# Queries and keys of a window attention block made with the tokens in another order

## The reference, cut to what matters

```python
xn = layernorm(x, ln1_w, ln1_b)
xs = jnp.roll(xn, shift=(-3, -3), axis=(1, 2))
xw = xs.reshape(B, H//7, 7, W//7, 7, C).transpose(0, 1, 3, 2, 4, 5).reshape(-1, 49, C)
qkv = xw @ qkv_w + qkv_b                     # (windows, 49, 3*192)
q, k, v = ...                                # each (windows, 6 heads, 49, 32)
attn = softmax(jnp.einsum('bhqd,bhkd->bhqk', q, k) * scale)
o = jnp.einsum('bhqk,bhkd->bhqd', attn, v) @ proj_w + proj_b
x = x + roll(unwindow(o), (3, 3))
h = gelu(layernorm(x, ln2_w, ln2_b) @ mlp_w1 + mlp_b1)
x = x + (h @ mlp_w2 + mlp_b2)
```

## Time and profile before

| what | value |
|---|---|
| time before, median of 3 runs | 3240.66 us (3238.58 to 3244.01) |
| the profiled execution: its own time | 3234.78 us |
| its span, first to last instruction | 3233.0 us |
| mean granted TensorE clock | 0.995 of full speed |
| TensorE busy (matmuls) | 3174.8 us, 98% of the span |
| VectorE, ScalarE, GpSimd busy | 69%, 62%, 22% |
| one step of the loop | about 24.8 us |

### The profile page before, as it was taken

The page is one execution under the profiler, slowest core; times in us unless marked ns, Lnnn a source line. Parts: engine busy times, 40 slices in busy tenths (PEclk is TensorE's granted clock), DMA queues, the critical chain, the costliest instruction groups (busy, mean ns, idle before and its releaser), DMA issues.

```text
span 3233.0 us, 110732 instructions
## 1 busy us (share of the span) xinstructions
PE 3174.8 (98%) x43444; PEld 2651.3 (82%) x43444; DVE 2227.1 (69%) x5903; ACT 2020.4 (62%) x3595; POOL 696.9 (22%) x785
## 2 busy tenths in 40 slices
PE   6999999999999999999999999999999999999998
PEld 6888888888888888888888888888888888888886
DVE  4677667666766676677667766766677667666764
ACT  3666666666666666666666666666666666666665
POOL 1222222222222222222222222222222222222221
PEclk8999999999999999999999999999999999999999
DMA  1010001000100010001000100000010001000100
GB/s 44 24 28 24 22 22 28 24 22 22 29 23 22 24 27 23 22 25 27 23 22 25 27 22 22 26 26 22 22 28 25 22 22 28 24 22 22 28 24 17
DMA packets 112096, 79.78 MB, mean 25 GB/s; under 512 B 10079, under 2 KB 111553, under 8 KB 112065
## 3 DMA queue, kind: packets, MB, share of 16 engines
q1 hardware_dynamic: 112064, 79.35, 9.3%
HBM read 40.78 MB, written 38.54 MB: 25 GB/s over the span
## 4 chain that ended last, share of the span: by engine, by line
PE 95%; ACT 3%; issue 1%; POOL 0%; DVE 0%; DMA 0%; SPq 0%; POOLq 0%; DVEq 0%; ACTq 0%
PE ps L743 31%; PE ps L810 16%; PE ps L746 15%; PE ps L818 8%; PE ps L778 5%; PE ps L841 5%; PE ps L861 4%; ACT vt L618 3%; PE ps L706 3%; PE ps L827 2%; PE ps L714 2%; PE ps L826 2%; PE ps L716 1%; DMA xin<-in_x 0%; POOL xb L362 0%
## 5 line engine op out<-in xcount | busy, mean ns | idle before, releaser
L743 PE MATMUL ps<-zh,w 128*128 128x392 f32 x3072 | 666.8, 345 | 22.1 <-ACT vt L618 21.4
L743 PEld LDWEIGHTS ps<-zh,w 128*128 128x128 f32 x3072 | 535.9, 188 | 63.2 <-ACT vt L618 62.4
L810 PE MATMUL ps<-g,w 128*128 128x392 f32 x1536 | 562.4, 502 | 0.0
L630 ACT ACTIVATE yT<-ps,b 128x392 f32<-128x392 f32 x256 | 150.5, 588 | 468.5 <-PE ps L818 424.4
L810 PEld LDWEIGHTS ps<-g,w 128*128 128x128 f32 x1536 | 271.4, 190 | 151.3
L743 PE MATMUL ps<-zh,wqkv 128*128 128x400 f32 x1536 | 391.7, 363 | 0.0
L666 ACT ACTIVATE g<-ps,biasf 128x392 f32<-128x392 f32 x768 | 386.2, 567 | 3.0 <-PE ps L743 1.1
L743 PEld LDWEIGHTS ps<-zh,wqkv 128*128 128x128 f32 x1536 | 281.2, 190 | 79.6 <-issue 77.0
L370 POOL TENSOR_TENSOR ve<-mv,eps 98x4 f32<-98x4 f32 x256 | 51.0, 199 | 1340.7 <-DVE mv L404 1340.7
L253 POOL TENSOR_TENSOR prob<-prob,rcp 128x588 f32<-128x588 f32 x128 | 152.2, 1189 | 867.7 <-DVE rcp L523 867.7
L412 DVE TENSOR_SCALAR z<-x,mv,rs 98x192 f32<-98x192 f32 (+2 forms) x768 | 208.6, 343 | 186.5 <-POOL rs L372 186.5
(11 more groups left out here) (94 smaller groups left out, 6021.0 us busy)
## 6 DMA issues: line engine op xcount, KB each, us to landing
xin<-in_x SPq DMA_DIRECT2D x128, 147.0 KB
out<-yo SPq DMA_DIRECT2D x128, 147.0 KB
xin<-in_x SPq DMA_DIRECT2D x128, 71.2 KB
out<-yo SPq DMA_DIRECT2D x128, 71.2 KB
xin<-in_x SPq DMA_DIRECT2D x128, 54.8 KB
out<-yo SPq DMA_DIRECT2D x128, 54.8 KB
xin<-in_x SPq DMA_DIRECT2D x128, 18.8 KB
out<-yo SPq DMA_DIRECT2D x128, 18.8 KB
```

The lines of the kernel that those rows point to most:

```text
L743: last = pe.matmul(dst, cols(w, part), act_ if zh is zh2 else windows(act_, WIDE, EVEN), start=(n == 0), stop=(n == 4))
L810: last = pe.matmul(ps[:, Y[0], 0:M], w2[:, k, 0:A], g[:, k, :], start=(k == 0), stop=(k == KC - 1))
```

## The change

The tokens of q and k get another order. In the moving operand of `qk` the token number is now the outer index and the window the inner one: `by_token` gives 49 runs of 8 columns, where neighbours within a run are 64 elements (256 bytes) apart in SBUF, and the next run begins one element further than the last one did. The result has 392 columns, with token t of window w at column 8t+w. ScalarE's four instructions take 392 columns where they took 400, and write them contiguously, as before. The scores then read the tokens of one window with a step of 8 elements (32 bytes): q, stationary, 64 columns, and k, moving, 49 columns. The q buffers are 512 columns wide, so GpSimd's one-off zeroing at the start covers 120 columns in place of 14. The number and the order of the instructions on every engine stay as they are: a step of TensorE still has 15 products in `qk` (now 128x392) and 48 in `s` (still 64x49).

```diff
-EVEN = TOK + 1
-N = WIN * EVEN
+N = WIN * TOK
@@
-        qA = sb("qA", [128, N + WIDE - EVEN])
-        qB = sb("qB", [128, N + WIDE - EVEN])
+        qA = sb("qA", [128, COLS])
+        qB = sb("qB", [128, COLS])
@@
+        def by_token(cols):
+
+            return cols.rearrange("p (w t) -> p t w", t=WIDE)[:, 0:TOK, :]
+
@@ in project
-                        last = pe.matmul(dst, cols(w, part), act_ if zh is zh2 else windows(act_, WIDE, EVEN),
+                        last = pe.matmul(dst, cols(w, part), act_ if zh is zh2 else by_token(act_),
@@ in s
-                                c0 = (4 * half + 2 * e + w) * EVEN
+                                win = 4 * half + 2 * e + w
                                 for n, h in enumerate(heads):
                                     r = slice(row + 32 * n, row + 32 * n + 32)
-                                    last = pe.matmul(ps[64 * e:64 * e + 64, S[h], at:at + TOK], q[r, c0:c0 + WIDE],
-                                                     k[r, c0:c0 + TOK], start=True, stop=True)
+                                    last = pe.matmul(ps[64 * e:64 * e + 64, S[h], at:at + TOK], q[r, win:COLS:WIN],
+                                                     k[r, win:N:WIN], start=True, stop=True)
```

## The result

The changed kernel takes 3709.93 us (median of 4 runs, 3705.51 to 3711.33), the kernel before 3240.61 us; the ratio is 1.1445, with a 95% interval of 1.1425 to 1.1465. It is slower by 469 us. The forecast was slower, at 3535 us; the range (3205 to 3720 us) holds the time, near its upper end.

A forecast was written before the change was run, and what follows sets the result against it. TensorE's stream was taken to bound the kernel; 2.31 us more per step in qk x 128 = 296 us, with the scores and other engines at nothing, gave 3531 us, 3537 in the median's terms, predicted as 3535 us (range 3205 to 3720).

The forecast's parts named there:

- What bounds the kernel: Whole kernel: TensorE, busy 98% of the span, sets the time; no slack in front of qk or the scores.
- likeliest case: Half rate in qk, scores as before: 3480 to 3600 us, chance 0.45.
- rival C: Scores: their stepped reads go at half the present rate, 166 us on top of qk as forecast, 3701 us; chance 0.12.
- The moving operand of `qk`: In qk: one column in two cycles, 344 ns a product instead of 190, 2.31 us more in a step.
- The upper bound of 0.96 ns for a jump: In qk: if every column step cost 0.96 ns, a product takes 555 ns, a step 5.5 us more.
- difference of 6.7 ns: Beyond its columns a qk product is 6.7 ns longer than an mlp1 product, possibly from its 7 jumps.
- rival D: In qk: every column pays 0.96 ns as a jump does, 700 us more, 3941 us; chance 0.08.
- The scores: Score stage: k's stepped read costs 0, as 41 ns for 49 columns is already one column in two cycles.
- under the same cover: Score stage: q's 64-column loads lie beside other heads' products, so no cost of their own is added.
- ScalarE, VectorE, GpSimd at nothing: Other engines: ScalarE saves at most 12 ns per activation, beside TensorE's work; nothing gained or lost in time.
- A (full rate): In qk: TensorE takes the jumping operand at full rate, -10 ns a product, 3221 us; chance 0.22.
- B: In qk: a price per run, 48 wraps of 0.96 ns, 226 ns a product, 69 us more, 3310 us; chance 0.09.

The follow-up runs named there:

- e11: Kernel before, with the moving operand of qk in 8 runs of 50 columns, 32 bytes between neighbours, real token order left out: 3519.2 us, ratio 1.087.
- e13: Kernel before, with the moving operand of qk in 56 runs of 8 columns, 32 bytes between neighbours, 448 columns: 3594.0 us (one run, beside 3236.7).
- e9: Kernel before, with the moving operand of qk in 4 runs of 98 columns, 16 bytes between neighbours, 392 columns: 3547.1 us, ratio 1.096.
- e6: Kernel before, with 392 contiguous columns as the moving operand of qk, no jump, last window left out: 3217.7 us, ratio 0.994.
- e14: Kernel before, with the moving operand of qk in 8 runs of 52 neighbours, 416 columns: 3234.0 us (one run, beside 3236.7).

## Why the prediction was right, and where it missed

*What bounds the kernel.* Right: TensorE's stream alone; no new wait, the clock as before, and 465 of the 469 us are in the two stages that were named.

*The number.* Part of it is luck. The forecast holds 296 us of the 469, and its own likeliest case, 3480 to 3600 us, does not reach the 3710. The range does, because its upper end was set for rival C. Two terms were too small, and both misses went the same way.

*The moving operand of `qk`.* The rate was right: two cycles a column, 344 ns forecast and 367 measured. The step was 2.31 us in the prediction and 2.71 in the chain, so it was mis-sized by 0.40 us, 51 us in all. Of the 40 ns that a product has beyond two cycles a column the prediction had 17; the missing 23 ns are 0.35 us in a step. e11 and e13, with 32 bytes in place of 256, are within 7 ns of two cycles a column. The ground for choosing that rate was weaker than it looked. The 355 ns of `mlp2_wide` are the distance of two records, and an F32 product has two of them: the code makes 6 products in a step where the trace has 12 records. So one column in two cycles was the pace of a record, and a whole F32 product went at half of that. It took e9 to e11 to show that two cycles is the rate of a jumping F32R operand.

*The upper bound of 0.96 ns for a jump.* The difference of 6.7 ns was real (e6), its reading was not: e14 keeps the jumps and loses the excess. The bound was built on the wrong cause. It did no harm to the forecast, since the half rate was taken, but rival D with its 3941 us had no ground.

*The scores.* This step failed. The prediction set them at 0, since a record of 49 columns in 41 ns "is already one column in two cycles", so that a read at that rate would not slow it down. The stage went from 1.30 to 2.22 us, 118 us. The 41 ns were the mean over a stretch with slower passages in it (from the fifth to the sixth set 158 ns pass); where the sets follow each other steadily, a record of a row range took 29 ns, 0.60 ns a column, and had room to lose. Both reads slow down: k alone makes the stage 1.72 us, the load of q alone 2.14. And q was put "under the same cover" without a price of its own, though it has 64 columns to k's 49; at 60 ns a load it is no longer covered by the 41 ns, and it gives most of the length. Rival C, at 3701 us, comes close to the time, but for a reason that is partly wrong: it doubled the stage (1.30 us more) by k's stream and kept 344 ns in `qk`. Its two errors (0.38 us too much for the scores, 0.40 too little for `qk`) cancel.

*The rest.* ScalarE, VectorE, GpSimd at nothing: right. A (full rate) is out by the 367 ns themselves and by e9 to e11; B is out by e13.

## What to carry to other kernels

In this kernel a moving F32R operand streamed at a column per cycle only where it came in groups of four neighbours; every other order that was tried, even pairs or every second element, cost a second cycle per column, 150 ns and more on a product of 190. A pad that keeps the runs contiguous is cheap beside that (8 columns, 3 ns), and runs of 52, a multiple of four, paid nothing for their jumps (187 ns for 416 columns). Where the order has to change, change it on an engine with time to spare and in its reads from PSUM, or make a compact copy, and price both operands of each product that reads the result, the stationary one too.

## What the runs showed that I had not expected

- Two neighbours out of four are worth nothing: 380 ns for 400 columns in pairs, 347 ns for 392 at a step of 8 bytes, 227 ns for 416 in fours.
- Wraps between runs cost nothing: 378 ns for 448 columns in 56 runs of 8 (373 at two cycles a column).
- Both operands of the small F32 products slow down when they are read with a step of 32 bytes: the score stage went from 1.30 to 1.72 us through the moving operand and to 2.14 us through the stationary one, and in its steady part both went to 0.94 ns a column, from 0.60 and 0.45.
- ScalarE's reads of PSUM with a step of 32 bytes are free (584 to 599 ns), its writes to SBUF with that step are not (975 to 1080 ns in place of about 590).
